# Mixing stage of a two-layer sequence kernel: outputs one step later, state turned in the outputs' bank, u spread by ScalarE

## What is computed

```python
value = silu(conv(x @ W_value)); u = value.reshape(.., H, DH)
bc = value @ W_bc                       # Bz, Bx, Cz, Cx for each head, each normalised to length 1
z = S * (z - dt * A * s + dt * Bz * u)  # one time step, S = 1/(1 + dt*k + dt*dt*A)
s = s + dt * z + dt * Bx * u
y = Cz . z + Cx . s
out = ((y + skip * value) * silu(gate)) @ W_out
```

## Time and profile before

| | us |
|---|---|
| median of three runs | 1326.06 |
| the profiled execution, whole | 1331.72 |
| its span, first to last instruction | 1329.6 |
| first `products` to last `take` (the mixing) | 217.9 to 637.8 |
| busy over the span: TensorE / its weight loads | 1279.4 / 705.5 |
| VectorE / ScalarE / GpSimd | 910.6 / 651.5 / 588.8 |

### The profile page before, as it was taken

How to read it: one execution, slowest core, us unless ns; L and a number is a source line. 1 busy time by engine, 2 the same in 40 slices (tenths; PEclk the granted TensorE clock), 3 DMA queues, 4 the chain that set the end, 5 groups by cost and what they waited for, 6 DMA issues and landing times. The chain is left out here.

```text
span 1329.6 us, 23001 instructions
## 1 busy us (share of the span) xinstructions
PE 1279.4 (96%) x7802; PEld 705.5 (53%) x7802; DVE 910.6 (68%) x1771; ACT 651.5 (49%) x1564; POOL 588.8 (44%) x939
## 2 busy tenths in 40 slices
PE   7999998999999999998899998999999999999999
PEld 4443334566566566565445454555655556544545
DVE  6999996999999999997301206888787786630100
ACT  3265533566665665664322315665565666531221
POOL 2633323888888988987100002444444453500000
PEclk7989999999999999998899999999999999999999
DMA  3369897656656665664100002000000000000000
GB/s 99 127 264 394 338 393 273 215 191 224 201 201 212 220 203 196 223 213 167 64 0 0 1 0 90 1 1 1 1 1 1 2 1 1 1 0 0 16 0 16
DMA packets 72834, 151.38 MB, mean 114 GB/s; under 512 B 7312, under 2 KB 24336, under 8 KB 69904
## 3 DMA queue, kind: packets, MB, share of 16 engines
q1 hardware_dynamic: 66096, 133.66, 28.5%
q10 hardware_dynamic: 6624, 16.26, 3.2%
HBM read 98.78 MB, written 51.12 MB: 113 GB/s over the span
## 5 line engine op out<-in xcount | busy, mean ns | idle before, releaser
L1869 POOL TENSOR_SCALAR pr<-pr,rs,sg 128x512 f32<-128x512 f32 (+3 forms) x256 | 152.6, 614 | 204.9 <-DVE rs L1774 186.1
L720 PE MATMUL banks<-w_bc,valueT 128*128 128x512 f32 x392 | 185.1, 596 | 3.4 <-ACT ent L593 2.4
L1046 DVE TENSOR_TENSOR pp<-banks,ring 128x1024 f32<-128x1024 f32 x128 | 156.1, 1220 | 12.8 <-DVEq L1083 5.5
L1675 ACT ACTIVATE pr<-banks,nm 128x512 f32<-128x512 f32 (+3 forms) x256 | 132.8, 524 | 20.4 <-DVE nm L1768 17.7
L1663 ACT COPY prT<-banks 128x512 f32<-128x512 f32 (+3 forms) x128 | 54.3, 424 | 112.5 <-PE banks L1544 112.3
L1768 DVE TENSOR_REDUCE nm<-banks 128x2 f32<-128x1024 f32 (+3 forms) x128 | 105.5, 824 | 4.4
L1384 DVE TENSOR_TENSOR x<-x,banks 128x256 f32<-128x256 f32 x16 | 6.7, 421 | 148.3 <-PE banks L1295 148.3
L935 ACT COPY qk<-banks 128x512 f32<-128x512 f32 x128 | 74.8, 585 | 63.0 <-PE banks L834 63.0
L672 POOL TENSOR_TENSOR C<-abL,A 128x128 f32<-128x128 f32 x128 | 53.3, 424 | 104.9 <-DVE banks L347 91.8
L1544 PE MATMUL banks<-ident,pr 128*128 128x128 f32 x640 | 96.9, 281 | 2.1 <-POOL pr L1869 0.7
L1130 POOL TENSOR_SCALAR_AFFINE_SELECT bp<-bp 128x1024 f32<-128x1024 f32 x64 | 73.8, 1152 | 55.9 <-ACT bp L942 55.9
(11 more groups left out here) (254 smaller groups left out, 2499.6 us busy)
## 6 DMA issues: line engine op xcount, KB each, us to landing
ring<-psi SPq DMA_DIRECT2D x126, 512.0 KB, 4.4
psi<-ring SPq DMA_DIRECT2D x10, 2048.0 KB, 7.5
psi<-X SPq DMA_DIRECT2D x5, 2048.0 KB, 7.5
det<-w_bc ACTq DMA_DIRECT2D x16, 512.0 KB, 4.7
ring<-det SPq DMA_DIRECT2D x64, 128.0 KB, 4.7
bcs<-ent ACTq DMA_DIRECT2D x30, 256.0 KB, 6.9
ring<-bcs SPq DMA_DIRECT2D x30, 256.0 KB, 5.0
w_bc<-in_w_bc SPq DMA_DIRECT2D x4, 1024.0 KB, 10.9
```

The source lines that it names most:

```text
L720: mm = pe.matmul(bank, m["valueT"][:, c, t * P:(t + 1) * P], w, start=(c == 0), stop=(c == 1))
L1046: dve.tensor_tensor(pp[:, q % 2].rearrange("p (a c) n -> p a c n", c=2), sc.unsqueeze(2).broadcast_to([P, 4, 2, HN]), rec[:, n % RL, q % 2 ...
L1675: act.activation(pr[:, n % RP, h, 0:w], S[n % 2][:, h, 0:w], ACT.Exp, bias=nm[:, n % 4, h:h + 1], accum_out=sm[:, m % 3, n % 2, h:h + 1]). ...
L1869: pool.tensor_scalar(row, row, rs[:, n // 2 % 2, n % 2, h:h + 1], sg[:, TPB * b + it, hd:hd + 1], ALU.mult, ALU.mult).then_inc(s["scaled"], 1)
```

## The change

TensorE makes `outputs(2p-2)` and `outputs(2p-1)` in step `p`, straight behind `scores(2p+1)`; the loops run one step longer. `turn_state` and `project_out` go from odd to even steps, behind the first `turn_both` and `project` of the step, and write columns 192 to 447 of bank YG instead of TP; they wait for `take` (`ygc`) instead of for a `copy_qk`. The waits of `turn_both` on `hz` and `oc` go, those at `outputs` take their place. On ScalarE `take` goes to even steps, between `root` and the first `copy_qk`; `spread_state` and the copy of `oc` go between the two `copy_qk`; `expand_u` comes from GpSimd to ScalarE, behind `square`, in every fourth step.

```diff
@@ -730,6 +730,7 @@
     RL, RB, RC, RQ = 3, 3, 2, 4
     LEAD = 4
     DIAG = P + DH
+    STATE = 2 * N + P
     with ExitStack() as ctx:
         sb, sem = tools(nc, ctx)
         w_out = sb("w_out", P, 2, D)
@@ -821,12 +822,6 @@
                 pe.wait_ge(s["bt"], q + 1)
                 if q >= 1:
                     pe.wait_ge(s["qk"], q)
-                if q >= 10 and q % 4 == 2:
-                    t, f, j = split(q - 7)
-                    if passes_on(t):
-                        pe.wait_ge(s["hz"], 2 * (links(t, f) + 1))
-                    if f == 1:
-                        pe.wait_ge(s["oc"], t + 1)
                 for pair in range(2):
                     pe.transpose(TP[:, pair * P:(pair + 1) * P],
                                  ct[:, q % RC, 2 * pair:2 * pair + 2].rearrange("p i n -> p (i n)"), k.ident[:])
@@ -853,8 +848,12 @@
                     pe.wait_ge(s["uz"], 2 * t + 3)
                     if q > 0:
                         pe.wait_ge(s["ygc"], q // 4)
-                    if carried(t):
-                        pe.wait_ge(s["hz"], 2 * (links(t - 1, f) + 1))
+                    if q >= 8:
+                        ts, fs, js = split(q - 8)
+                        if passes_on(ts):
+                            pe.wait_ge(s["hz"], 2 * (links(ts, fs) + 1))
+                        if fs == 1:
+                            pe.wait_ge(s["oc"], ts + 1)
                 for i in range(4):
                     row = slice(32 * i, 32 * i + 32)
                     mm = pe.matmul(YG[row, 0:2 * N + P], uz[:, t % 2, f, P * j + 32 * i:P * j + 32 * i + 32], bp[:, q // 2 % RB, :, q % 2, i],
@@ -873,39 +872,38 @@
 
             def turn_state(t, f):
                 pe.wait_ge(s["hT"], links(t, f) + 1)
-                pe.transpose(TP[:, 0:P], hT[:, f].rearrange("p a n -> p (a n)"), k.ident[:]).then_inc(s["turned"], 1)
+                pe.transpose(YG[:, STATE:STATE + P], hT[:, f].rearrange("p a n -> p (a n)"), k.ident[:]).then_inc(s["turned"], 1)
 
             def project_out(t):
                 pe.wait_ge(s["yg_done"], 2 * t + 2)
                 if t == 0:
                     pe.wait_ge(s["o_loaded"], 16)
                 for f in range(2):
-                    mm = pe.matmul(TP[:, P:2 * P], yg[:, t % 2, f], w_out[:, f], start=(f == 0), stop=(f == 1))
+                    mm = pe.matmul(YG[:, STATE + P:STATE + 2 * P], yg[:, t % 2, f], w_out[:, f], start=(f == 0), stop=(f == 1))
                 mm.then_inc(s["out"], 1)
 
             pe.sem_inc(s["bc"], 4)
             for _ in range(2):
                 pe.matmul(SE[:], k.ident[:], m["valueT"][:, 0, 0:4 * P])
-            for p in range(2 - LEAD, PAIRS + 2):
+            for p in range(2 - LEAD, PAIRS + 3):
                 if 0 <= p < PAIRS:
                     scores(2 * p)
                     scores(2 * p + 1)
+                if 1 <= p <= PAIRS:
+                    outputs(2 * p - 2)
+                    outputs(2 * p - 1)
                 for u in range(2):
                     if 0 <= p + 1 < PAIRS:
                         turn_both(2 * p + 2 + u)
                     if 2 <= p + LEAD < PAIRS:
                         project(2 * (p + LEAD) + u)
-                if 0 <= p < PAIRS:
-                    outputs(2 * p)
-                if p >= 3 and p % 2 == 1:
-                    t, f, j = split(2 * (p - 2))
-                    pe.wait_ge(s["qk"], min(2 * p + 4, UNITS))
-                    if passes_on(t):
-                        turn_state(t, f)
-                    if f == 1:
-                        project_out(t)
-                if 0 <= p < PAIRS:
-                    outputs(2 * p + 1)
+                    if p >= 4 and p % 2 == 0 and u == 0:
+                        t, f, j = split(2 * (p - 4))
+                        pe.wait_ge(s["ygc"], min(p, PAIRS) // 2)
+                        if passes_on(t):
+                            turn_state(t, f)
+                        if f == 1:
+                            project_out(t)
 
         @block.scalar
         def _(act):
@@ -957,10 +955,18 @@
                 act.wait_ge(s["yg"], HG * t + 4 * f + 4)
                 for l in range(2):
                     lane = slice(64 * l, 64 * l + 64)
-                    src = TP[lane, 0:P].rearrange("p (a l j d) -> p a l j d", a=2, l=2, j=4)[:, :, l]
+                    src = YG[lane, STATE:STATE + P].rearrange("p (a l j d) -> p a l j d", a=2, l=2, j=4)[:, :, l]
                     dst = hz[lane, f].rearrange("p (j e) -> p j e", e=DIAG)[:, :, 0:P].rearrange(
                         "p j (a l e) -> p l a j e", a=2, l=2)[:, l, :, :, 0:DH]
                     act.copy(dst, src).then_inc(s["hz"], 1)
+
+            def expand_u(t):
+                act.wait_ge(s["yg"], HG * (t - 1))
+                for f in range(2):
+                    dst = uz[:, t % 2, f].rearrange("p (j e) -> p j e", e=DIAG)[:, :, 0:P].rearrange(
+                        "p j (i e) -> p j i e", i=4)[:, :, :, 0:DH]
+                    act.copy(dst, m["u"][:, t, f * P:(f + 1) * P].rearrange("p (i j d) -> p j i d", i=4, j=4)
+                             ).then_inc(s["uz"], 1)
 
             def moments(t):
                 act.wait_ge(s["x"], t + 1)
@@ -977,18 +983,17 @@
 
             act.sem_inc(s["sq"], 2)
             act.sem_inc(s["root"], 2)
-            for p in range(2 - LEAD, PAIRS + 2):
+            for p in range(2 - LEAD, PAIRS + 3):
                 if 0 <= p < PAIRS:
                     copy_scores(p)
                 if 2 <= p + LEAD - 1 < PAIRS:
                     root(p + LEAD - 1)
+                if 2 <= p <= PAIRS and p % 2 == 0:
+                    take(p // 2 - 1)
                 if 0 <= p + 1 < PAIRS:
                     copy_qk(2 * p + 2)
-                    copy_qk(2 * p + 3)
-                if 2 <= p + LEAD < PAIRS:
-                    square(p + LEAD)
-                if p >= 3 and p % 2 == 1:
-                    t, f, j = split(2 * (p - 2))
+                if p >= 4 and p % 2 == 0:
+                    t, f, j = split(2 * (p - 4))
                     if f == 1:
                         act.wait_ge(s["out"], t + 1)
                     if passes_on(t):
@@ -996,9 +1001,13 @@
                     if f == 1:
                         if t > 0:
                             act.wait_ge(s["x"], t)
-                        act.copy(oc[:], TP[:, P:2 * P]).then_inc(s["oc"], 1)
-                if 0 <= p < PAIRS and p % 2 == 1:
-                    take(p // 2)
+                        act.copy(oc[:], YG[:, STATE + P:STATE + 2 * P]).then_inc(s["oc"], 1)
+                if 0 <= p + 1 < PAIRS:
+                    copy_qk(2 * p + 3)
+                if 2 <= p + LEAD < PAIRS:
+                    square(p + LEAD)
+                if p >= 4 and p % 4 == 1 and p // 4 + 1 < TILES:
+                    expand_u(p // 4 + 1)
                 b, i = divmod(p - 20, 16)
                 if 0 <= b < B - 1:
                     if i < TPB:
@@ -1107,8 +1116,6 @@
         def _(pool):
             def expand_u(t):
                 for f in range(2):
-                    if t >= 2:
-                        pool.wait_ge(s["yg"], HG * (t - 1))
                     dst = uz[:, t % 2, f].rearrange("p (j e) -> p j e", e=DIAG)[:, :, 0:P].rearrange(
                         "p j (i e) -> p j i e", i=4)[:, :, :, 0:DH]
                     pool.tensor_copy(dst, m["u"][:, t, f * P:(f + 1) * P].rearrange("p (i j d) -> p j i d", i=4, j=4)
@@ -1164,8 +1171,6 @@
                     combine(2 * p + 4)
                 if p >= 7 and p % 4 == 3:
                     residual(p // 4 - 1)
-                if p >= 4 and p % 4 == 1 and p // 4 + 1 < TILES:
-                    expand_u(p // 4 + 1)
                 if p >= 28 and p % 16 >= 12:
                     normalise(TPB * (p // 16 - 1) + p % 16 - 12)
             residual(TILES - 1)
```

## The result

The changed kernel takes 1353.02 us (median of four runs, 1347.57 to 1359.66) where the kernel before takes 1328.85 (four runs): ratio 1.0186, with 95% between 1.0153 and 1.0219. It is slower by 24 us; the forecast of 1319.8 and its range up to 1331 are missed, and on the other side of no change.

What follows compares the result with a forecast made beforehand. TensorE's own order was taken to bound carried tiles. From 1326.1 us, -9 (state's detour) + 9 (bare waits) - 3.3 (small waits) - 3.0 (end) = -6.3 gave 1319.8, own range 1315 to 1325, wider range 1311 to 1331.

Steps and rivals of the forecast that it cites:

- VectorE's holding: VectorE's L1023 waiting out a GpSimd instruction: 2.02 us in a 26.00 us tile, taken to stretch and shrink with the step.
- What bounds the kernel: Mixing, carried tiles: TensorE's own order is the bound, 25.46 of 26.00 us; VectorE without holding needs 23.98.
- The detour of the state: TensorE, turn_state and project_out: moved behind a projection they save 0.67 us a tile, about -9 us.
- Outputs behind the scores: TensorE, odd steps: same work, but outputs no longer cover the wait for the qk copy, +9 us.
- The bare wait: TensorE, before the second unit's scores: 0.25 to 0.3 us uncovered on each of 32 odd steps, +9 us.
- Small waits: TensorE: outputs no longer wait for their own mask (6.5 us), turns give combine more time (10.8 us); -3.3 us counted.
- ScalarE: ScalarE: expand_u adds 6 to 9 us off the path; the mask comes up to 0.6 us later, unseen by TensorE.
- The loop through `take`: Rival, 10%: root waits for reduce, take and the qk copy queue behind on ScalarE; slower, 1335.
- The end: Behind the last projection: scores(62) and scores(63) no longer wait for outputs and the state's detour, -3.0 us.
- The base: Starting time: median 1326.06 us, taken as the run without the 4.80 us L1055 of the profiled execution.
- VectorE is the bound: Rival, 25%: holding stays, VectorE needs 6.50 us a step, steady state gains nothing, only the end's 3.0: 1323.
- The signs: Trace after: four carried steps in about 25.4 us, L1023's mean near 0.5; wrong if over 25.9 or under 25.

Runs made afterwards that it cites:

- late mask: Changed kernel with root ahead of the two score copies on ScalarE on odd steps, so GpSimd's mask starts later: 1322.61 us, ratio 0.9952 to the kernel before.
- the first experiment: Changed kernel with state and evacuate ahead of the step's reduce on VectorE, not behind it: 1320.52 us, ratio 0.9936 to the kernel before.
- the repeated run: Kernel before with only the state's turn and project_out moved into the outputs' bank YG, measured once more: 1321.95 us, ratio 0.9951 to the kernel before.

## Why the prediction was wrong

The step that failed is the one that took VectorE's holding as given (0.50 us a step, on L1023 alone) and let the mask's new time cost nothing: "TensorE doesn't see it". The runs show holding go from 31.9 to 54.0 us (33.9 more on `state` and `evacuate`, 11.8 less on L1023), and the mixing longer by 21.6. With the collision out of the way the whole change is worth -8.6 us (`state` ahead of `reduce`) or -6.7 (late mask) by the medians. That the sum gave -6.3, so near to them, is in part luck: the detour gave less than forecast, and what the small waits gave isn't known.

- *What bounds the kernel.* TensorE's starts were read rightly, and where the collision is absent they hold: tiles of 25.40, 25.37 and 25.09. The sentence that failed is "VectorE stretches to fill the step, up to a point". The point was never worked out. An estimate from the stretches: VectorE without holding needs 27.37 - 4.70 = 22.7 us of busy time in a tile, and sits idle for some 1.4 (28.81 - 27.37; before, 1.3); under TensorE's 25.4 that leaves room for some 1.3 us of holding. The tile of before has 1.5, the changed one 4.70.
- *The detour of the state*: mechanism right, size nearly. 0.67 us a tile were forecast, 25.48 - 25.09 = 0.39 measured; -9 in all, -7.8 measured. By the starts of the scores, before and with only the state in YG, the two odd steps of the twelfth tile give back 1.36 us, with 1.32 forecast (1.76 - 0.44). The two even ones take 0.94 where 0.65 was forecast: the mis-sized term is what `turn_state` and `project_out` cost in their new place.
- *Outputs behind the scores*: this is where the collision was left out. I asked what TensorE has bare without the outputs as cover, and not when the scores' consumer on GpSimd would now run and beside what. The bare wait itself is there, in 32 places as forecast. The scores behind an odd step take 522.28 to 523.67 = 1.39 us from their start to the next group's, where the others and nearly all of before take 1.10: 0.29 more, with 0.25 to 0.3 forecast, and 9.3 us over 32 steps for the forecast 9. The first experiment carries it, and its tile is 0.31 us above that of the kernel with only the state in YG.
- *Small waits*: the turns and outputs did wait less for GpSimd. In the view of the earlier trace rows the changed kernel has 2.4 and 2.2 us left of the 10.8 and 6.5, but there TensorE waits for products instead; the first experiment has 6.4 and 2.2. So 8.7 of 17.3 us are gone in a kernel without the collision; how much of that shortened it was not separated, and -3.3 can't be read from it.
- *ScalarE*: right that `expand_u` is free, shown three times over. The 4 us at most by which VectorE might gain from it don't show: with `expand_u` alone moved holding is 31.2 for 31.9. Wrong that a later mask doesn't matter, but in the other direction: it would have helped.
- *The loop through `take`*: it was the rival with the right sign and the wrong mechanism. It put the price on L1023, which in fact fell from 24.9 to 13.1 us of holding, while the instructions of `state` and `evacuate` went from 7.0 to 40.9.
- *The end*: last `products` to last `take` is 14.7 us before, 11.2 after, 10.1 in the first experiment and 13.3 with only the state in YG. The last two differ by 3.2, which agrees with -3.0; they differ in the outputs' shift, but also in the places of `take`, `expand_u` and `state`.
- *The base.* I took the 4.80 us instruction of the earlier trace rows for an event of one execution. It comes back at the same place in three other kernels (below), and it doesn't explain the distance from the profiled execution to the median. The granted clock goes with that distance. Of 35 runs of the kernel before, the four with a mean clock of 0.990 or 0.991 took 1322.1 to 1323.3 us, and the six at 0.979 or 0.980 took 1332.9 to 1335.5. The profiled one had 0.981, and 909.7 us outside the mixing. With `expand_u` alone moved the mixing took the same (419.6 us) and the rest 905.8, at 0.988.
- *VectorE is the bound* (25%) was the better rival, priced at nothing lost since I let the holding "stay what it is". The rule of the Trainium skill named beside it (Perfetto Trace Analysis, on the most-contended engine) pointed right: by it VectorE, not TensorE, is to be asked first, and here it had 27.37 of 28.81. SBUF — State Buffer of the Trainium skill (the section SBUF: two separate sides) says that the loser is blocked for the winner's whole instruction; the 1.11 us of L1068 up to the end of the mask agree. I had used it to price `expand_u`, 4 us at most, and not on the state.
- *The signs.* The one that came true is "over 25.9 (VectorE or the loop)", with 28.81; moving `root` says that it is VectorE. The mean of L1023 did not stay near 0.5: it is 0.397.

## What to carry to other kernels

An edit that lets one engine run earlier moves the phase of everything behind it: list the short VectorE instructions that work in SBUF, above all those with two inputs, and ask beside which GpSimd instruction each will now start. Here four in a row were held by four GpSimd instructions one after the other. Where a shift makes a kernel slower and no wait explains it, compare mean durations of equal instructions before and after first, and then test by moving the victim or by delaying the aggressor; either was one small edit here. A busy share doesn't tell work from holding (VectorE's was 95% before and after). A wait that grows on the way (here `root` on `reduce`) is to be taken away once before it is believed.

## What the runs showed of the hardware

Holding looks the same in most places read: a VectorE instruction of 0.29 us takes as long as GpSimd's goes on and ends 0.13 to 0.15 us after it, although the next one of GpSimd starts at once (519.36 to 522.13 above). It isn't only for instructions with two inputs: the copy `gs` (L1066, one input, 0.184 us undisturbed) took up to 1.14 us in the changed kernel. One place is otherwise. With only the state in YG, late in the mixing:

```profile
606.75 4.79 DVE L1055 TENSOR_TENSOR gs<-ygc,hT 128x64 f32<-128x64 f32 x1
606.88 0.73 POOL L1145 TENSOR_TENSOR bp<-pp 128x256 f32<-128x256 f32 x1
...
607.56 0.73 POOL L1150 TENSOR_TENSOR ct<-ct,ring 128x256 f32<-128x256 f32 x1
608.23 1.15 POOL L1130 TENSOR_SCALAR_AFFINE_SELECT bp<-bp 128x1024 f32<-128x1024 f32 x1
...
610.73 0.73 POOL L1150 TENSOR_TENSOR ct<-ct,ring 128x256 f32<-128x256 f32 x1
...
611.44 0.45 POOL L1124 TENSOR_SCALAR gateT<-x,mx_nmean,mx_rstd 128x128 f32<-128x128 f32 x1
```

A `gs` of 0.21 us ends at 611.54, past six GpSimd instructions that start back to back; it is 4.80 us before, 4.79 again in the repeated run, 4.78 with the state in YG and ahead of `reduce`, 4.80 with the late mask, and 2.70 in the kernel before with only `expand_u` moved. In the changed kernel this instruction (L1064) is never over 1.10 us, and with `state` ahead of `reduce` never over 0.51. Why it is passed over here, and an instruction behind it isn't elsewhere, no run tells apart.
